# An attention and expert kernel on one core: another setup, another order of its steps, and identity matmuls on PE

## The reference

```python
x = x + conv(ln_c(x))                 # attention with 8 heads of 16 channels
t = x.reshape(B, 768, 128)
x = t + ffn(ln_t(t))                  # 8 experts of width 512

# conv: all 768 tokens of a batch attend to all others
q, k, v = xf @ Wq, xf @ Wk, xf @ Wv
att = q @ k.T / 4 + bias_t + bias_p   # biases by distance in time and in part
att = where(causal in time, att, -inf)
y = softmax(att) @ v @ Wo

# ffn: two rounds, with the larger and the smaller of the two best gate weights
for i in range(2):
    w_in = x * top_p[..., i]
    h = gelu(w_in @ W1[e] + b1[e]); out += h @ W2[e] + b2_sum
```

## Time and profile before

| | us |
|---|---|
| median of 3 runs | 2416.75 |
| lowest, highest | 2404.98, 2417.44 |
| the profiled execution, own time | 2419.99 |
| its span, first to last instruction | 2418.2 |
| PE busy in it | 2177.8 (90%) |
| ACT busy | 1622.5 (67%) |
| DVE busy | 1283.4 (53%) |
| POOL busy | 1041.9 (43%) |

### The profile page before, as it was taken

The page is one execution under the profiler, slowest core; times in us unless marked ns, Lnnn a source line. Parts: engine busy times, 40 slices in busy tenths (PEclk is TensorE's granted clock), DMA queues, the critical chain, the costliest instruction groups (busy, mean ns, idle before and its releaser), DMA issues.

```text
span 2418.2 us, 46619 instructions
## 1 busy us (share of the span) xinstructions
PE 2177.8 (90%) x17445; PEld 1978.6 (82%) x17445; DVE 1283.4 (53%) x3190; ACT 1622.5 (67%) x2728; POOL 1041.9 (43%) x1049
## 2 busy tenths in 40 slices
PE   1578999899999989999998999999999998999998
PEld 0457888788888888888888888888888887888898
DVE  2235475454646545474654547456454754546453
ACT  3227767677676667767676776767677676776776
POOL 2104354344434434453443445434444543444366
PEclk8568999999999999999999999999999999999999
DMA  3512122040212204022120402203031220402200
GB/s 47 88 42 34 21 35 29 11 50 12 34 25 34 31 8 54 6 34 29 28 37 8 53 6 35 30 17 47 8 41 17 36 29 11 50 10 32 27 5 8
DMA packets 69290, 70.29 MB, mean 29 GB/s; under 512 B 20334, under 2 KB 54346, under 8 KB 69066
## 3 DMA queue, kind: packets, MB, share of 16 engines
q1 hardware_dynamic: 68850, 67.25, 19.8%
q10 hardware_dynamic: 216, 0.08, 0.0%
HBM read 10.83 MB, written 6.29 MB: 7 GB/s over the span
## 4 chain that ended last, share of the span: by engine, by line
PE 64%; ACT 15%; DVE 11%; issue 4%; POOL 2%; SPq 2%; DMA 0%; ACTq 0%; DVEq 0%; POOLq 0%
PE acc L885 19%; PE wide L814 6%; PE wide L799 6%; PE wide L824 6%; PE zps L874 6%; PE zps L876 6%; PE zps L875 5%; ACT z L514 5%; ACT h L540 4%; ACT h L539 2%; POOL h L455 2%; DVE maxes L656 2%; PE wide L838 2%; DVE h L719 2%; PE wide L846 2%
## 5 line engine op out<-in xcount | busy, mean ns | idle before, releaser
L455 POOL TENSOR_TENSOR h<-h 128x384 f32<-128x384 f32 x1024 | 1019.9, 1007 | 1289.7 <-ACT h L540 1279.4
L539 ACT ACTIVATE h<-zps,b_col 128x384 f32<-128x384 f32 x1024 | 591.2, 577 | 485.3 <-DVE h L719 441.1
L885 PE MATMUL acc<-w,h 128*128 128x128 f32 x6144 | 852.7, 281 | 0.0
L885 PEld LDWEIGHTS acc<-w,h 128*128 128x128 f32 x6144 | 823.9, 197 | 2.0
L719 DVE TENSOR_TENSOR h<-zps,ratio_b 128x384 f32<-128x384 f32 x1024 | 536.0, 549 | 493.3 <-PE zps L876 478.8
L656 DVE TENSOR_REDUCE maxes<-wide 128x1 f32<-128x128 f32 (+5 forms) x768 | 431.7, 614 | 409.7 <-PE wide L799 407.0
L540 ACT ACTIVATE h<-h,b_col 128x384 f32<-128x384 f32 x1024 | 621.3, 607 | 0.0
L874 PE MATMUL zps<-x_hi,w_lo 128*128 128x384 f32 x1024 | 392.5, 383 | 57.3 <-DVE x_lo L698 40.1
L514 ACT ACTIVATE z<-wide 128x896 f32<-128x896 f32 (+2 forms) x384 | 336.0, 916 | 58.2 <-PE wide L814 50.5
L814 PE MATMUL wide<-stack 128*128 128x256 f32 (+3 forms) x1280 | 278.5, 349 | 83.3 <-ACT z L514 54.2
L876 PE MATMUL zps<-x_hi,w_hi 128*128 128x384 f32 x1024 | 351.2, 343 | 0.0
(11 more groups left out here) (95 smaller groups left out, 1205.7 us busy)
## 6 DMA issues: line engine op xcount, KB each, us to landing
stack<-halves SPq DMA_DIRECT2D x384, 96.0 KB, 3.1
stack<-halves SPq DMA_DIRECT2D x384, 24.0 KB, 2.6
x_in<-in_x SPq DMA_DIRECT2D x128, 48.0 KB, 2.4
out_dram<-outt SPq DMA_DIRECT2D x256, 24.0 KB, 1.6
w<-in_L_ffn_W SPq DMA_DIRECT2D x8, 256.0 KB, 4.0
stack<-max_rows SPq DMA_DIRECT2D x128, 3.0 KB
stack<-max_rows SPq DMA_DIRECT2D x128, 1.5 KB
stack<-z SPq DMA_DIRECT2D x6, 192.0 KB
```

The source lines that it names most:

```text
L455: pool.tensor_tensor(h1[:, PLACE[m], :], h0[:, m % 2, :], h1[:, PLACE[m], :], ALU.add).then_inc(hsum_ready, 1)
L539: act.activation(h0[:, m % 2, :], zps[BANK[m]][:, 0:CT], ACT.Gelu, bias=b1_col[:, j:j + 1]).then_inc(h0_ready, 1)
L885: ins = pe.matmul(acc[:, n * P:(n + 1) * P], h1[:, PLACE[k], n * P:(n + 1) * P], w2[:, j, :], start=(j == 0 and n == 0), stop=(j == UNITS_ ...
```

## The change

Three things are changed.

Setup. The first batch's x is loaded from two queues, four DMAs on SP and four on ACT. The time table goes by six small DMAs into the rows of the stack's partitions, unspread (t_rows). ACT copies rows 32 to 63 of it, spread, into the stack (`spread_low`, group 0 ahead of batch 0's steps, group 1 behind value 0). DVE (group 0) and POOL (group 1) spread rows 64 to 127 and add the part table on the way (`spread_high`). The twelve wide DMAs are gone. W1 and Wo are loaded behind the last copies of the second group of heads, and W1 is split in two behind mix 0.

Order. FIRSTS and all slots are redrawn.

Identity matmuls. `idle` issues matmuls of the identity by itself: three into the wide buffer ahead of the first scores of each group, five that add into a part of acc's bank that is not read behind the second part of the first head, and eight into the wide buffer ahead of the split. By these lines a batch has 3 + 3 + 5 + 5 + 8 = 24 of them.

```diff
-AT = {("stats", 0): -5.5, ("seed", 0): -5.0, ("root", 0): -3.5, ("scale", 0): -3.5, ("turn", 0): 0, ("query", 0): 1.0,
+AT = {("stats", 0): -6.5, ("seed", 0): -5.0, ("root", 0): -5.0, ("scale", 0): -3.5, ("turn", 0): 0, ("query", 0): 0.5,
...
+        def spread_high(eng, g, n):
+            t0, t1 = ((0, TOK), (TOK, QW))[n]
+            turns = (t1 - t0) // PARTS
+            eng.tensor_tensor(qst[64:P, g * GH:(g + 1) * GH, t0:t1].rearrange("p h (t n) -> p h t n", n=PARTS),
+                              window(t_rows[64:P, :], (TIMES - 1) * HEADS + g * GH, [[1, GH], [-HEADS, turns], [0, PARTS]]),
+                              window(p_hl, (PARTS - 1) * HEADS + g * GH, [[1, GH], [0, turns], [-HEADS, PARTS]]),
+                              ALU.add).then_inc(high_spread[g], 1)
...
-            load_x(0)
+            load_x(0, range(TPT // 2))
...
-            sp.wait_ge(pool_set, POOL_KEYS)
+            sp.wait_ge(pool_set, POOL_SMALL)
+            sp.wait_ge(tables_low, 2)
+            for n, row in enumerate(TIME_ROWS):
+                for half in range(2):
+                    sp.dma_start(t_rows[row + half * TPT:row + (half + 1) * TPT, 0:(TIMES - n * TPT) * HEADS],
+                                 t_hl[32 * half:32 * half + TPT, n * TPT * HEADS:]).then_inc(bias_rows, 16)
+            sp.wait_ge(pool_set, POOL_SET)
...
-                            sp.dma_start(qst[rows, :, 0:TOK].bitcast(F32), src[:, :, at:at + TOK]).then_inc(bias_placed, 16)
-                            sp.dma_start(qst[rows, :, TOK:QW].bitcast(F32), src[:, :, at:at + HALF]).then_inc(bias_placed, 16)
+                if (step, a) == ("stack", (1, GH - 1)):
+                    for e in range(EXPERTS):
+                        sp.dma_start(w1_stage[:, e, :], W1[e]).then_inc(w1_loaded, 16)
...
-                elif (step, a) == ("stack", (0, GH - 1)):
-                    for e in range(EXPERTS):
-                        sp.dma_start(w1_stage[:, e, :], W1[e]).then_inc(w1_loaded, 16)
...
+            for tl in range(TPT // 2, TPT):
+                act.dma_start(x_in[tl * PARTS:(tl + 1) * PARTS, :, :],
+                              x[0].rearrange("n (i t) c -> t n i c", t=TPT)[tl]).then_inc(x_loaded, 16)
...
+            def spread_low(g):
+                for t0, t1 in ((0, TOK), (TOK, QW)):
+                    act.copy(qst[32:64, g * GH:(g + 1) * GH, t0:t1].rearrange("p h (t n) -> p h t n", n=PARTS),
+                             window(t_rows[32:64, :], (TIMES - 1) * HEADS + g * GH,
+                                    [[1, GH], [-HEADS, (t1 - t0) // PARTS], [0, PARTS]])).then_inc(low_spread, 1)
...
                 if (step, a) == ("value", 0):
+                    spread_low(1)
+                elif (step, a) == ("mix", 0):
                     for a in range(2):
...
-            act.wait_ge(tables_low, 2)
-            for g in range(GROUPS):
-                act.copy(qst[64:111, g * GH:(g + 1) * GH, :].rearrange("p h (t n) -> p h t n", n=PARTS),
...
+            act.wait_ge(bias_rows, 16 * BIAS_DMAS)
+            spread_low(0)
...
+                    if hh == 0 and part == 0:
+                        idle(w[:, 0:P], 3)
...
+                    if hh == 0 and part == 1:
+                        idle(acc[:, CT:CT + P], 5, start=False)
...
+                    if a == 0:
+                        idle(w[:, 0:P], 8)
                     pe.wait_ge(xn_ready, r.at(4, 3 + a))
...
+            def idle(to, count, start=True):
+                for _ in range(count):
+                    pe.matmul(to, ident[:, :], ident[:, :], start=start, stop=start, skip_group_check=not start)
```

More of the change, by code:

```diff
@@ L51 @@
 MAX_ROW = 127
-PAD = 2 * P
 LN_EPS = (1e-6, 1e-5)
@@ L339, in prepare @@
             def prepare(r, step, a):
-                if (step, a) == ("value", 0):
-                    sp.wait_ge(times_spread, 1)
-                    sp.wait_ge(parts_spread, GROUPS)
-                    sp.wait_ge(pool_set, POOL_SET)
-                    for n, to in enumerate(TIME_ROWS):
-                        for half in range(2):
-                            rows, src = slice(to + half * TPT, to + (half + 1) * TPT), spread[32 * half:32 * half + TPT]
-                            at = PAD - n * P
-                            sp.dma_start(qst[rows, :, 0:TOK].bitcast(F32), src[:, :, at:at + TOK]).then_inc(bias_placed, 16)
-                            sp.dma_start(qst[rows, :, TOK:QW].bitcast(F32), src[:, :, at:at + HALF]).then_inc(bias_placed, 16)
+                if (step, a) == ("stack", (1, GH - 1)):
+                    for e in range(EXPERTS):
+                        sp.dma_start(w1_stage[:, e, :], W1[e]).then_inc(w1_loaded, 16)
                     for h in range(HEADS):
@@ L415, in _ @@
             cleared = ((wo_pad[:, :, :], 0.0), (ident[:, :], 0.0), (hot_stage, 0.0), (pick[:, :], 0.0),
-                       (twos, 2.0), (average, 1.0 / C), (ones, 1.0), (t_hl, 0.0), (p_hl, 0.0))
+                       (twos, 2.0), (average, 1.0 / C), (ones, 1.0), (t_hl, 0.0), (p_hl, 0.0), (t_rows, 0.0))
             later = ((kst[32:64, :, :].bitcast(F32), 0.0), (kst[64:P, :, :].bitcast(F32), 0.0),
-                     (spread[0:40, :, 0:PAD], 0.0), (val[:, :, :, HD:2 * HD], 1.0))
+                     (val[:, :, :, HD:2 * HD], 1.0))
             done = 0
@@ L449, in _ @@
             assert done == POOL_SET
+            pool.wait_ge(pool_set, POOL_SET)
+            pool.wait_ge(tables_low, 2)
+            pool.wait_ge(bias_rows, 16 * BIAS_DMAS)
+            pool.wait_ge(xn_ready, 2)
+            for n in range(2):
+                if n:
+                    pool.wait_ge(high_spread[1], n)
+                spread_high(pool, 1, n)
             pool.sem_inc(hsum_ready, NH0)
@@ L458, in prepare @@
             def prepare(r, step, a):
-                if (step, a) == ("value", 0):
+                if (step, a) == ("mix", 0):
+                    pool.wait_ge(high_spread[1], 2)
                     for a in range(2):
@@ L512, in attention @@
                         act.wait_ge(wide_filled[n % 2], r.at(WPB, n // 2 + 1 - (WPB if g == 0 else 0)))
+                    if r.b == 0 and g == 0 and hh == 0 and part == 0:
+                        for n in range(GROUPS):
+                            act.wait_ge(high_spread[n], 2)
                     z0, z1 = ((0, 896), (896, 1664), (1664, ZW))[part]
@@ L751, in prepare @@
                     pe.wait_ge(hots_placed, 16 * HOT_DMAS)
-                    pe.wait_ge(parts_spread, GROUPS)
-                    pe.wait_ge(bias_placed, 16 * BIAS_DMAS)
+                    pe.wait_ge(low_spread, 2)
+                    pe.wait_ge(high_spread[0], 2)
+                elif (step, a) == ("scores", (0, GH - 1, 2)):
+                    pe.wait_ge(low_spread, 4)
+                    pe.wait_ge(high_spread[1], 2)
                 elif (step, a) == ("divide", 1):
```

49 lines of the change are left out of this document (24 added, 25 removed).

## The result

The changed kernel takes **2375.1 us** (median of 4 runs, 2370.4 to 2376.9) against 2417.1 us of the kernel before on the same chip: a ratio of 0.983, with a 95% interval of 0.981 to 0.985. The forecast was 2400, a gain of 0.7%; the gain is 1.7%. The profiled execution took 2375.36 us with a span of 2373.6, so 44.6 us of span are to be placed.

The account below looks back on a forecast made before the run. It took the start as bound by a chain of dependent steps, the steady part by PE's work, waits and half clock. Start -35 and fifteen batches at +1.2 (+18) gave -17 us: 2400 us, range 2360 to 2428.

Parts of the forecast that it names:

- The start: Setup before the steady batches: earlier copies -31.7, act_t -2, rows step -4.2, identities +3, in all -35 us (-28 to -41).
- Group 0: First head group of each batch: identities delay it 0.6 us, the held clock gives 0.84, net -0.2 us a batch.
- 0.6 us of delay is left: First head group: eight identities take 1.76 us, waits there hide all but 0.6 us a batch (bounds 0 and 1.0).
- Group 1: Second head group: identities and moved units fill 2.77 us of waits, clock holds (0.8), 0.6 comes back; net -1.4 us a batch.
- The split: Split of x in each batch: 2.65 us later, -0.94, +1.76 for moved units, -0.67; +2.8 us a batch (1 to 4).
- the third wait: PE's wait after the first units behind the split: goes as Vector reaches its next products sooner, 0.67 us a batch.
- -0.94: From the split to the first unit: 4.29 us becomes 3.35, as in batch 0 at half clock, per batch.
- the clock after the split I leave as it was: Behind the split: identities cannot hold the clock over the transposes, so half clock there stays, no gain counted.
- (1): Rival: the split is not late and costs nothing; -1.6 us a batch, 2358 us, chance 0.17.
- (2): Rival: split late, but identities keep the clock up over it, saving 1.65 us a batch; 2375 us, chance 0.12.
- (3): Rival: long wait before the split lowers the clock in transposes and a second stretch; +3.5 us a batch, 2434 us, chance 0.13.
- (4): Rival: the start gains only 10 us, as new rows arrive late or ACT's spread is slow; 2425 us, chance 0.08.

Follow-up runs that it names:

- e3b: The changed kernel without any of the identity matmuls, run for its trace: 2389 us, ratio 0.988 to the kernel before.
- e4: The changed kernel without the eight identities ahead of the split, all else kept: 2380.5 us, ratio 0.986.
- e8: As e5, without the eight identities ahead of the split: 2358.0 us, ratio 0.977.
- e2: The changed kernel with the order of before, identities kept: 2378.9 us, ratio 0.984.
- e5: The changed kernel with Vector's statistics and seed behind the step that makes xn, roots behind x_lo: 2359.0 us, ratio 0.977.
- e1: The changed kernel with the order of before and no identities, so the rebuilt setup alone: 2378.8 us, ratio 0.986.
- e6: As e5, but statistics, seed and roots of the batch after next all behind both splits' x_lo: 2389.3 us, ratio 0.990.
- e9: As e5, with the root steps and next xn behind the products of z64 and z65 in Vector's queue: 2364.3 us, ratio 0.980.

## Why the prediction was too small

The mechanism was right in the start, in group 1 and ahead of the split. Three terms of the sum were mis-sized: the stretch behind the split by 1.4 us a batch, group 0 by 0.7, and the last batch, which was taken like the others, by 5.3 in all. The first is the step that failed: it counted one fall of the clock twice.

**The start: right, with some luck.** -35 was forecast, -33.6 is in the trace, and the setup alone gives -34 in the times. But only 27.4 us of it stand at batch 0's rows step, and the rest lies in the stretch that varies by 5.5 us. Inside it terms missed each other. The copies came 27.6 us sooner, not 31.7, as Vector's spread, which was to lie "in the time in which it waits for ACT", took 16.55 us. ACT's copy of act_t came 5.1 us sooner (21.82 for 26.94), not 2, since ACT's spread of group 0 took 4.12 us where the old rate gave 8.7, and ACT takes the rows step's transpose at once, 62.12 behind 61.71. The cost of a spread on GpSimd, 26 us estimated from ACT's rate, is 12 us alone; that GpSimd and Vector wait for each other wasn't in the sum at all.

**Group 0: there was more room than the sum saw.** "0.6 us of delay is left" did not come. From group 0's rows step to group 1's it is 49.26 us in every batch, the 49.3 of the batches before whose clock did not fall. The order made 0.57 us of room there (e3b has 48.73), and the eight fill 0.53 of it. The clock's part, 0.84, came, and in this order without their help. Net -0.9 where -0.2 was forecast.

**Group 1: right.** From its rows step to its mix it is 18.54 us on average instead of 20.31, -1.77, forecast -1.4, and here it is the identities that hold the clock, as e3b shows (19.49 without them).

**The split: late as forecast, but one fall of the clock was counted twice.** Ahead of the split nearly every number held: PE ready 8.1 us after the issue (8.4), the split at 13.6 (13.5), a wait of 5.4 less 1.76 of identities, so 3.6 (3.3), the third wait gone. From group 1's rows step to the issue it is 37.9 us (668.97 to 706.87), where it was 739.76 - 702.42 = 37.3: +0.6, forecast -1.4 + 1.76 = +0.36. From the issue to the split +2.8, forecast +2.65. But from the split to the next rows step there were 795.17 - 750.62 = 44.55 us, and now there are 41.6 on average: -3.0, where -0.94 - 0.67 = -1.61 was forecast. This is the term that was mis-sized, by 1.4 us a batch, some 20 us in fourteen, and the two pairs of windows above say why. From the split to the first unit it is 3.5 us on average (2.6 to 3.8) instead of 4.29: -0.8, near the -0.94. From the first unit to the next query it is 7.83 instead of 9.87: -2.04, of which the third wait is 0.6 (9.4 us in all, now 1.4), another 0.2 is the wait for act_t, and 1.2 are the clock: 0.83 over 9.87 us is 1.7 us lost before, where it is 0.5 now on average and none in the window shown. The -0.94 had been taken from batch 0 at half clock, so it already held a fall over the transposes (batch 15 of the changed kernel, with nothing in Vector's way and no fall, has 2.36 us there); and then "the clock after the split I leave as it was" left the units at half clock too. One fall was counted twice. Before the change it fell on the units, now it falls on the transposes and on the one second unit behind them, where a part of the stretch had been a wait anyway.

From group 1's to the next group 0's rows step that gives +0.4 on average instead of +1.4.

**The last batch.** The sum took fifteen batches alike. Batch 15 has no x to load for a later one, so no statistics stand ahead of its split: it has the gains alone, -4.1 us where +1.2 was written.

So: start +1.4 against the forecast, fourteen batches 14 x (-0.49 - 1.2) = -23.7, the last -5.3, in all -27.6, which is 2403.0 - 2375.4.

**The rivals.** (1), a split that isn't late, is refuted: it is late as forecast. (2), that the identities keep the clock up over the split, is refuted: it fell in every batch. By e4 they put it off a little, worth 0.35 us a batch, and by e8 they are worth nothing once the wait is short. The time that (2) gave, 2375, is the measured one, and for another reason: that is luck.

By the Trainium skill (TensorE: Matmul & The Clock Gate, Part 4 (PE-mode transpose)) a transpose does not count as PE-busy in the way a matmul does, and the prediction drew from it that identities ahead of the transposes cannot hold the clock over them. The changed kernel looks like it, but a wait of 3.6 us stands between, so it does not test the rule. Where no long wait stands there the clock is 1.00 as the twelve transposes run, in all 14 batches, with identities ahead of them (e2, e5) and without (before, e1, e8). So identities don't decide it in these runs; what sets the changed kernel apart from these is the wait.

(3), two stretches of half clock, came in part: the clock is low for 6.8 us in 5 of the 14 batches, from 0.9 to 1.6 us ahead of the split on. It cost less than the price set for it, as from the split to the next rows step these five have 41.8 us and all fourteen 41.6 on average; with one wait of 4.8 us (e6) the 6.8 us came in all 14. (4) is refuted by e1.

**What stays open.** Whether the 3 us of start between e1 and the changed kernel belong to the order: the start varies by more than that. Why order alone is 10 us slower in the times and not in the traces, which are one execution each. And how long one piece of waiting may be: no run changes that alone, since each edit that cuts a wait also moves it.

## What to carry to other kernels

A wait removed by reordering one queue can come back a few instructions later in about the same length, as it did here from xn to x_lo and h (e5) and from h to the next xn (e9). What can still be won is its shape: here 3.6 us in one piece cost 1.25 us a batch more than the same time in two pieces with matmuls between. And when work is moved, write down the wait that it leaves and also the one that it enters.

## What the runs showed that was not expected

- Vector and GpSimd, both on additions with two inputs in repeated and transposed reads, took turns instruction by instruction, so that running at once gained nothing: 16.55 and 20.37 us together, 8.92 and 11.97 us one behind the other.
- Filler matmuls pay only where the clock would fall: 0.9 us for eight in group 1, minus 0.5 for the same eight in group 0, nothing at the split when its wait is short.
- Two kernels with the same instructions there differ by 5.5 us in their start (127.6 and 133.1 us from the first to the second rows step), with the clock low for 41 and 55 us of it.
